# Second attention of a two-layer block on one Trainium2 core: value matmuls in four blocks per group, or in one

## What is computed

```python
q = (x @ Wq.T).reshape(B, T, 16, 8).transpose(0, 2, 1, 3) * (1.0 / 8) ** 0.5
k, v = ...                                   # 4 heads, each used by 4 query heads
scores = jnp.einsum('bhqd,bhkd->bhqk', q, k)
dist = jnp.clip(pos[None, :] - pos[:, None], -127, 127) + 127
scores = scores + jnp.einsum('bhqd,kqd->bhqk', q, E[dist])
attn = jax.nn.softmax(scores, axis=-1)
out = jnp.einsum('bhqk,bhkd->bhqd', attn, v)
```

## Time and profile before

| what | value |
|---|---|
| median of 3 runs | 1612.63 us (1611.99 to 1632.21) |
| the profiled execution | 1619.09 us, span of its instructions 1617.4 us |
| busy in the span: PE, DVE, ACT, POOL | 1357.1, 893.8, 813.2, 661.8 us |
| first to last exponential of the second attention | 984.5 to 1547.4 us |

### The profile page before, as it was taken

The page is one execution under the profiler, slowest core; times in us unless marked ns, Lnnn a source line. Parts: engine busy times, 40 slices in busy tenths (PEclk is TensorE's granted clock), DMA queues, the critical chain, the costliest instruction groups (busy, mean ns, idle before and its releaser), DMA issues. The chain is left out here.

```text
span 1617.4 us, 39052 instructions
## 1 busy us (share of the span) xinstructions
PE 1357.1 (84%) x14415; PEld 904.6 (56%) x14415; DVE 893.8 (55%) x2426; ACT 813.2 (50%) x1571; POOL 661.8 (41%) x1281
## 2 busy tenths in 40 slices
PE   3999899989998997317999158999989999999967
PEld 1577677737776776215667124555545555555545
DVE  4566556446665665680233255666666666667652
ACT  2455455545554554100322255667666767777643
POOL 1466566516665662017154413334333334334400
PEclk9999999989999998558999666989998999999978
DMA  5610000052000000621253336666666566566600
GB/s 180 97 22 2 2 2 2 2 106 52 2 2 2 2 2 1 211 93 60 57 98 75 61 102 197 181 190 194 198 177 183 165 174 181 170 188 180 175 1 27
DMA packets 112815, 154.24 MB, mean 95 GB/s; under 512 B 15011, under 2 KB 98339, under 8 KB 111339
## 3 DMA queue, kind: packets, MB, share of 16 engines
q1 hardware_dynamic: 105851, 146.91, 33.0%
q0 software_dynamic: 6784, 4.87, 2.3%
HBM read 84.98 MB, written 66.46 MB: 94 GB/s over the span
## 5 line engine op out<-in xcount | busy, mean ns | idle before, releaser
L435 ACT ACTIVATE t_Pt<-t_psT 128x512 f32<-128x512 f32 x512 | 278.8, 596 | 242.4 <-PE t_psT L329 242.4
L377 DVE CUSTOM_DVE_ANT_0 t_Z<-t_psS,a0b_L 128x1024 f32<-128x1024 f32 x256 | 310.1, 1220 | 156.3 <-issue 150.7
L863 ACT ACTIVATE t_Pt<-t_psT 128x512 f32<-128x512 f32 x512 | 288.1, 596 | 160.8 <-PE t_psT L677 92.1
L765 DVE TENSOR_REDUCE t_mm<-t_psS 128x1 f32<-128x640 f32 (+1 forms) x256 | 219.6, 858 | 203.2 <-DMA t_A<-relative_rows 137.0
L329 PE MATMUL t_psT<-idf,t_Z 128*128 128x128 f32 x2048 | 283.6, 283 | 19.8 <-POOL t_Z L400 13.6
L400 POOL TENSOR_SCALAR t_Z<-t_Z,t_m 128x1024 f32<-128x1024 f32 x256 | 286.8, 1120 | 0.0
L329 PEld LDWEIGHTS t_psT<-idf,t_Z 128*128 128x128 f32 x2048 | 224.7, 144 | 107.4 <-issue 40.3
L663 PE MATMUL t_psS<-a1b_KT,a1b_QT 72*128 72x512 bf16 (+3 forms) x672 | 214.8, 348 | 5.6 <-DVE t_mm L766 5.4
L706 PE MATMUL t_psO<-t_Pt,t_Vh 128*32 128x128 f32 x4096 | 171.2, 287 | 3.6 <-DVE t_Os L789 3.6
L288 PE MATMUL t_psS<-a0b_KT,a0b_QT 72*128 72x512 bf16 (+1 forms) x512 | 155.3, 385 | 5.1 <-PEq L76 3.3
L834 POOL TENSOR_SCALAR t_neg<-t_m 128x4 f32<-128x4 f32 x64 | 14.1, 221 | 329.0 <-DVE t_m L775 329.0
(11 more groups left out here) (329 smaller groups left out, 1460.7 us busy)
## 6 DMA issues: line engine op xcount, KB each, us to landing
relative_rows<-t_rows SPq DMA_DIRECT2D x256, 192.0 KB, 2.9
t_A<-relative_rows SPq DMA_DIRECT2D x192, 192.0 KB, 3.2
t_A<-relative_rows SPq DMA_DIRECT2D x64, 128.0 KB, 2.4
a1b_QT<-query_parts SPq DMA_DIRECT2D x24, 192.0 KB
x_B<-in_b SPq DMA_DIRECT2D x1, 4096.0 KB, 18.1
x_A<-in_a SPq DMA_DIRECT2D x1, 4096.0 KB
a0b_QT<-query_parts SPq DMA_DIRECT2D x6, 576.0 KB
a0b_KT<-key_parts SPq DMA_DIRECT2D x18, 192.0 KB
```

Of the source, the lines that this page charges most:

```text
L377: nc.vector.tensor_tensor_reduce(out=Z[:, j, :], in0=psS[:, j % 2, :], in1=L[:, qt, :], scale=1.0, scalar=3e38, op0=ALU.add, op1=ALU.min, ...
L435: nc.scalar.activation(Pt[:, qt % 2, j, half * (N // 2):(half + 1) * (N // 2)], psT[:, half, :], ACT.Exp).then_inc(s_exp, 1)
L765: v.reduce_max(mm[:, u % AR, 1:2], psS[:, u % 2, width:N], AX)
L863: nc.scalar.activation(Pt[:, q % PR, :], psT[:, unit_item(G, i) % RR, :], ACT.Exp).then_inc(s_exp, 1)
```

## The change

- The value matmuls of group G - 1, all 8 key tiles and 32 matmuls (64 records), stand in one block behind the second unit and the first relative tile of group G. In the version before four blocks of two key tiles stood behind units 1, 3, 5 and 7.
- So exponentials live for longer: 12 buffers in place of 6 (`PR`). Six of them are the two spent tiles `qp` and `kp`, three parts each, read as float32; six are in `Pt`, as before.
- ACT waits once, before the first exponential, until the stores out of `qp` and `kp` have landed.
- At the end the 8 value tiles of the last group stand in one block.

```diff
-    ZR, AR, PR, RR = 3, 8, 6, 3
+    ZR, AR, PR, RR = 3, 8, 12, 3
@@
-        Pt = ph.sb("Pt", [P, PR, J * P])
+        more = ph.sb("Pt", [P, PR - 2 * SPLIT, J * P])
+        Pt = [part[:, i, :].bitcast(F32) for part in parts for i in range(SPLIT)] + [more[:, i, :] for i in range(PR - 2 * SPLIT)]
@@ values
-                                                Pt[:, q % PR, j * P:(j + 1) * P], start=i == 0, stop=i == QT_N - 1)
+                                                Pt[q % PR][:, j * P:(j + 1) * P], start=i == 0, stop=i == QT_N - 1)
@@ tensor: for G, for i
                             if i == 1 and G >= 1:
-                                values(G - 1, 6)
-                                values(G - 1, 7)
-                            if i > 1 and G >= 0:
-                                values(G, i - 3)
-                                values(G, i - 2)
+                                for k in range(8):
+                                    values(G - 1, k)
@@ tensor: after the loop
-                values(GROUPS - 1, 6)
-                values(GROUPS - 1, 7)
+                for k in range(8):
+                    values(GROUPS - 1, k)
@@ scalar
+                            if q == 0:
+
+                                act.wait_ge(s_parts, 16 * 2 * SPLIT)
                             act.wait_ge(s_u, q + 1)
                             if q >= PR:
                                 act.wait_ge(s_pv, q - PR + 1)
-                            nc.scalar.activation(Pt[:, q % PR, :], psT[:, unit_item(G, i) % RR, :], ACT.Exp).then_inc(s_exp, 1)
+                            nc.scalar.activation(Pt[q % PR], psT[:, unit_item(G, i) % RR, :], ACT.Exp).then_inc(s_exp, 1)
```

More of the change, by code:

```diff
@@ L568, in _, with attend_direct @@
                 store(1, s_parts, s_parts)
-def attend_direct(nc, tag, QT, KT, V, attn, con, EBT, scratch, qd, kd, s_one, s_near, s_rest, s_last, s_parts):
+def attend_direct(nc, tag, QT, KT, V, attn, con, EBT, scratch, qd, kd, s_one, s_near, s_rest, s_last, s_parts, parts):
     PB, J, GRP = (H // 4) * QT_N, 4, 4
@@ L1955, in sandwich @@
             project_pair(nc, "p1", xn, w[:, 0:C], wk2[:], wv, QT, KT, V, idf, qd, kd, (qp, kp), con["ones"], s_one, s_near, s_parts, SCORE_SCALE, kb)
-            attend_direct(nc, "t1", QT, KT, V, y, con, EBT, scratch, qd, kd, s_one, s_near, s_rest, s_last, s_parts)
+            attend_direct(nc, "t1", QT, KT, V, y, con, EBT, scratch, qd, kd, s_one, s_near, s_rest, s_last, s_parts, (qp, kp))
         finish(nc, "f", y, wo, X, hT, W1, W2, out_rows, idf)
```

## The result

The changed kernel takes 1634.37 us (median of 20 runs), the kernel before 1620.38 us (median of 20 runs, in the same sessions). The ratio is 1.0091, interval 1.007 to 1.0113: a loss of 0.9%, some 14 us between the medians, clear of noise and small. The forecast was 1617 on a base of 1612.6, so +4; the changed kernel lies inside the range, the sign is right, the size was too small, and the loss does not come from where the forecast's sum has it.

What follows compares the result with a forecast made beforehand. Two close loops bound the stage: PE with ACT through three PSUM slots, and SyncE's stores and fetches. Group chain 0, DMA loop +8, low clock -5, end +1 make +4 on 1612.6: 1617 us, range 1590 to 1650.

Steps and rivals of the forecast that it cites:

- PE's saving of 0.71 us per group: Second layer's attention, value matmuls: one block for four saves 0.44 us after blocks and 0.27 us on ways in.
- ACT's hole: ACT before a group's third exponential: idle 1.86 us instead of 0.57, making a plain group 8.2 us instead of 7.68.
- The sum over the kinds: Mean over plain, fold, new-output-tile and first or last query-tile groups: 8.25 us before and after, so 0 per group.
- The DMA loop: SyncE's stores and fetches, closed through PE: a later second row copy lengthens the round, +8 us, bounds 0 and +16.
- +0.25 us each: Round of stores and fetches over two groups grows from 7.1 to some 7.6 us; charged to 32 of 64 groups.
- Low clock, -5 us: Stage's groups at 1.2 GHz, 4 groups' worth: PE alone bounds them, so its saving gives 1.2 us in each.
- New wait, 0: ACT's wait before the first exponential for six stores issued long before, at the projection's end: costs 0.
- the end, +1: Behind the last exponential the last value block stands alone, 1.95 us, where half was done before: +1 us.
- Rival C: PE stops at nearly every slot, so its clock falls: +20 us per another 56 us at 1.2 GHz; chance 0.10.
- Rival A: PE's drains decide: slots absorb ACT's idle time, 64 x 0.71 = 45 us saved, 1568 us; chance 0.12.
- rival B: Second copy of rows comes too late for SyncE's queue: 0.62 us in each group, +40 us, 1653; chance 0.14.
- clock clearly below 0.95: Sign that the forecast is wrong and Rival C holds: the attention stage's clock falls clearly under its 0.95.

Runs made afterwards that it cites:

- the run with eight: Changed kernel with its values in eight blocks of one key tile, one behind every unit; ratio 1.0123 to the kernel before.
- the spare matmuls: Changed kernel plus matmuls that compute nothing: four per group before the maxima, ratio 1.0030 to before; with eight more before the third relative matmul, 1.0077.
- The run behind the fourth unit: Changed kernel with its block of eight value tiles moved from behind the second unit to behind the fourth; ratio 1.0069 to the kernel before.
- the one with blocks behind units 4 and 6: Changed kernel with two blocks of four key tiles, behind unit 4 (unit 2 where an output tile begins) and unit 6; ratio 0.9968 to before.

## Why the prediction was right or wrong

- *PE's saving of 0.71 us per group, the price of a block of 0.24:* right. 0.26 and 1.89 us in the trace, 0.24 per block in the run with eight.
- *ACT's hole:* right, 1.88 us for 1.86. Plain groups 8.01 for 8.2, fold groups 8.7 to 8.8 for 8.9, the wait for the output copy gone, those groups 8.20 in the mean for 8.2. The sum over the kinds, 0 per group, was 0.1 to 0.2 us too high: the working's 8.25 for before was already below its own mean of 8.34, since it took undisturbed groups, and a part of ACT's hole falls where a group of before waited for a landing.
- *The DMA loop, +8 us:* wrong. The second store did become the one that waits, but the round was not longer: DVE's waits for landings fell (122.8 to 80.1 us, 95.0 in the second profile), and the groups at the full clock are not longer than before (8.27 and 8.35 us for 8.48 to 8.50). The step that failed is "+0.25 us each": it followed one way round the loop and assumed that no other wait in it would shrink.
- *Low clock, -5 us:* wrong, and this is the step that made the number too small. It priced PE's saving in stretches at 1.2 GHz and took their number as given. It grew: from 53.5 to 72.6 and 77.5 us in the stage of the profiles, and by 40 us over the whole program in the mean of the runs, +15 us of time at 0.38. The price was read from a group that is no typical one besides: the group of 12.80 us is the first of the stage, with 81 PE records where 96 is a full plain group, so 12.80 against 8.34 prices the low clock too low.
- *New wait, 0; the end, +1:* both a little too small: 1.3 us for the table load that now stands behind the unit, and 1 to 3 us at the end, by profiles whose other parts vary as well.
- *Rival C* named this mechanism, with a chance of 0.10 and +20 us for 56 us more at 1.2 GHz; it was +15 for 40. What spoke against it, a group of 8.74 us with PE idle for 1.28 and the clock at 1.00, was one group; its work around the stop was still dense. The Trainium skill's sentence (TensorE: Matmul & The Clock Gate, A second HAM failure mode: psum-queue depth-cycling), that brief, frequent idling between groups of matmuls makes the clock swing, agrees with the runs: eight of eleven falls behind stops of 0.41 to 1.04 us, and 0.899 against 0.910 as the mean clock. The rows of before could not show it, and I took that for a sign against it.
- *Rival A* (drains decide) fell with the plain group's 8.01; *rival B* with the groups at the full clock, which did not get longer, with SPq's waits for rows (48.9 for 46.6 us), and with the spare matmuls, which don't make the copy earlier and take two thirds of the loss away. The run behind the fourth unit agrees, though it pays for the output copy as well.
- Of the signs set down, "clock clearly below 0.95" was the right one to name. The profiled execution shows 0.94 only; it took the clocks of many runs to see it.

## What to carry to other kernels

Fewer changes of tiling mode are worth their 0.24 us only as long as TensorE was the engine that set the pace *and* stays busy; in a ring of three slots, one long block starves the engine that empties it, and where the block stands (in front of a one-matmul refill, or of four transposes) is worth as much as how many there are: 8.01, 7.34 and 7.26 us for the same work in an undisturbed group. Over all plain groups at the full clock, landings leave little of it: 8.11, 7.80 and 7.96 us. So take the mean over all groups, and not the cleanest one. When the time is set elsewhere anyway, work taken from TensorE can come back as clock: look at the mean clock of all runs, not at one profile, before and after.

## What the runs showed that was not expected

- Eight blocks, 62 us of added work on TensorE by the group's length, cost 20 us, since waits for landings and falls of the clock shrank with them: 0.9212 for 0.9113.
- Four spare matmuls of 192 columns per group, 256 in all, raise the program's mean clock from 0.899 or 0.900 to 0.9087 and make it faster by about 9 us.
- With one block behind the second unit, 14 of the 22 falls in two profiles have no stop over 1.1 us close ahead of them, the shortest stop 0.33 us; with the order of before, 2 of 18 falls in three profiles (1.04 and 1.06 us), the longest stop 2.74 us. That it is the sparse work around the stop that does it is my reading. What amount of activity decides was not measured and stays open, as does why versions with the same busy share in the stage (92% in the changed kernel and in the one with blocks behind units 4 and 6) differ, 0.900 to 0.908.
